# Second norm's columns by transposing transfers instead of TensorE, with logits one step later and the first and last steps reordered

## What is computed

```python
h = concat([tok(x), txt(x_txt)], axis=1)            # (64, 229, 128)
h = h + attn(layernorm(h))                          # gated attention, squared relu instead of softmax
t = layernorm(h)                                    # the second norm
shared = sum over 2 shared experts of gelu(t @ w1.T + b1) @ w2.T
logits = t @ gate_w.T + gate_b                      # 8 experts; softmax, top 2 of them
out = h + shared + sum over the top 2 of p_e * (gelu(t @ rw1[e].T + rb1[e]) @ rw2[e].T + rb2[e])
```

## Time and profile before

| | |
|---|---|
| median of 3 runs | 1225.05 us (1223.14 to 1229.79) |
| the profiled execution | 1222.94 us, of which its span is 1221.2 us |
| granted TensorE clock, mean | 0.991 of full speed |
| busy share | TensorE 95%, VectorE 80%, GpSimd 69%, ScalarE 66% |
| DMA traffic | 143.51 MB, 118 GB/s on average |

### The profile page before, as it was taken

How to read it: one execution, slowest core, us unless ns; L and a number is a source line. 1 busy time by engine, 2 the same in 40 slices (tenths; PEclk the granted TensorE clock), 3 DMA queues, 4 the chain that set the end, 5 groups by cost and what they waited for, 6 DMA issues and landing times.

```text
span 1221.2 us, 31914 instructions
## 1 busy us (share of the span) xinstructions
PE 1158.8 (95%) x9418; PEld 871.8 (71%) x9418; DVE 974.0 (80%) x2516; ACT 807.1 (66%) x1867; POOL 837.3 (69%) x808
## 2 busy tenths in 40 slices
PE   5899999999999999779999999999999999999998
PEld 3677777777777777654555458999999998965555
DVE  4688998888888888868977777777777766779997
ACT  2566656666765666645555547777777777768887
POOL 4335776666677777647878846777777777776664
PEclk9999999999999999989999999999999999999999
DMA  7134444444444442224344425554444544539998
GB/s 187 63 119 125 127 125 134 132 134 132 134 136 138 124 136 96 72 83 106 103 117 129 111 53 96 94 98 94 93 98 95 96 91 92 93 82 191 209 194 171
DMA packets 208055, 143.51 MB, mean 118 GB/s; under 512 B 119036, under 2 KB 186745, under 8 KB 207892
## 3 DMA queue, kind: packets, MB, share of 16 engines
q1 hardware_dynamic: 166868, 93.93, 30.6%
q0 software_dynamic: 36992, 40.97, 15.8%
q10 hardware_dynamic: 4032, 6.57, 2.1%
HBM read 70.38 MB, written 55.96 MB: 103 GB/s over the span
## 4 chain that ended last, share of the span: by engine, by line
PE 35%; POOL 34%; issue 21%; ACT 3%; SPq 2%; DVE 2%; DMA 2%; POOLq 0%; ACTq 0%; DVEq 0%
POOL slots_dram L487 9%; POOL slots_dram L1550 7%; PE bank L1838 4%; PE bank L1862 4%; PE bank L1861 4%; PE bank L1863 4%; PE bank L1840 4%; PE bank L1839 4%; POOL rstd L528 3%; POOL slots_dram L497 2%; POOL rstd L534 2%; POOL emb L457 2%; PE bank L1271 2%; PE bank L1310 2%; PE bank L1270 2%
## 5 line engine op out<-in xcount | busy, mean ns | idle before, releaser
L1561 POOL DMA_INDIRECT y_dram<-y_sb,y_row x244 | 268.8, 1102 | 98.3 <-issue 74.9
L1646 ACT ACTIVATE gel_all<-bank,b 128x256 f32<-128x256 f32 x488 | 191.4, 474 | 40.8 <-PE bank L1840 39.2
L1277 ACT ACTIVATE gel_all<-bank,b 128x458 f32<-128x458 f32 x256 | 154.4, 640 | 85.3 <-PE bank L1271 56.4
L1861 PE MATMUL bank<-w_part_hi,hid_all 128*128 x976 | 170.7, 219 | 0.0
L1863 PE MATMUL bank<-w_part_hi,hid_all 128*128 x976 | 169.7, 219 | 0.0
L1862 PE MATMUL bank<-w_part_lo,hid_all 128*128 x976 | 169.7, 219 | 0.0
L1768 DVE CAST hid_all<-gel_all 128x1024 f16<-128x1024 f32 x122 | 85.4, 700 | 97.4 <-ACT gel_all L1646 97.4
L487 POOL DMA_INDIRECT slots_dram<-row_bufs,slot_1st x128 | 131.8, 1030 | 41.0 <-issue 37.3
L1770 DVE TENSOR_TENSOR hid_all<-gel_all,hid_all 128x1024 f16<-128x1024 f32 x122 | 149.5, 1225 | 4.2
L1288 DVE TENSOR_TENSOR hid_all<-gel_all,hid_all 128x916 f16<-128x916 f32 x128 | 142.5, 1113 | 4.4
L1838 PE MATMUL bank<-xT_r,w_part_hi 128*128 128x256 f16 x488 | 133.3, 273 | 3.1 <-DMA tags_r<-slots_dram 2.8
(11 more groups left out here) (190 smaller groups left out, 3029.8 us busy)
## 6 DMA issues: line engine op xcount, KB each, us to landing
xin<-in_xmain SPq DMA_DIRECT2D x32, 771.8 KB
x2r_dram<-row_bufs SPq DMA_DIRECT2D x32, 260.0 KB, 2.1
x2t_dram<-x2T SPq DMA_DIRECT2D x32, 229.0 KB, 2.8
x_cols<-x2t_dram ACTq DMA_DIRECT2D x28, 229.0 KB, 3.2
row_bufs<-x2r_dram SPq DMA_DIRECT2D x24, 260.0 KB, 2.8
stage<-in_ffn_w SPq DMA_DIRECT2D x20, 256.0 KB
xin<-in_xrest SPq DMA_DIRECT2D x32, 128.6 KB
y_dram<-y_sb,y_row POOLq DMA_INDIRECT x244
```

The lines of the kernel that those rows point to most:

```text
L1561: pool.indirect_dma_start(out=y_dram, in_=y_sb[:, s, c, :], in_offset=None, out_offset=bass.IndirectOffsetOnAxis(ap=y_row[:, s, c:c + 1], ...
L1646: act.activation(gel[:, s8 % 2, f, :], up_bank[s8 % 2][half][:, (f % 2) * TILE:(f % 2 + 1) * TILE], ACT.Gelu, bias=of_expert(b1, SHARED * ...
L1861: pe.matmul(part, h_hi, w2_hi, start=False, stop=False)
```

## The change

The columns of the second norm no longer come from TensorE. `turn_x2` issues four transposing transfers per pair on SyncE's queue, from the fp16 row buffer in SBUF to the column tile in SBUF; the 128 transpositions of TensorE (`x2_columns`), 32 copies of ScalarE (`columns_hi`) and 32 subtractions of VectorE (`x2_low`) are gone. The block sizes swap to 112 and 117, and each image's columns get room for 240, so the column tile and its copy in DRAM grow from 458 to 480 numbers per row; `up` reads 2x229 of them. `halves_hi` and `halves_low` move ahead in their steps. `logits`, `top` and `choose` of a pair come one step later, `logits` stands right behind `av`; `rank` stays in its step, and `slots` moves to the end of VectorE's step. `top` gets two buffers (`mx8`). Steps -3 to -1 and 29 to 31 have orders of their own, with other pieces of the shared experts between them; TensorE turns `ident` 28 times while the first loads run, and ScalarE loads its Silu table at the start. VectorE's list behind step 30 is now: `halves_low(30)`, `middle(31)`, first `early.split`, `mid_shift(31)`, `top(29)`, `choose`, second `early.split`, `slots`, `halves_low(31)`, third `early.split`, `top(30)`, fourth `early.split`, `top(31)`, `choose`, `slots`. The core of the diff:

```diff
-CHUNKS = ((0, 117), (117, 112))
+CHUNKS = ((0, 112), (112, 117))
...
+IMG_COLS = CHUNKS[1][0] + P
+PAIR_COLS = 2 * IMG_COLS
+TURN_ROWS = (CHUNKS[0][1], P)
...
-            def store_x2(b, parity, buf):
+            def turn_x2(b, parity, buf):
+                if reaches(b, 2):
+                    sp.wait_ge(lg_done, b - 1)
+                    sp.wait_ge(t_out[parity], 8 * (b - parity))
                 sp.wait_ge(rows_ready, b + 1)
+                for img in range(2):
+                    for c, (at, _) in enumerate(CHUNKS):
+                        n, col = TURN_ROWS[c], img * IMG_COLS + at
+                        sp.dma_start(x2T16[:, parity, :, col:col + n], rows_16[0:n, buf, 2 * img + c, 0:2 * HID],
+                                     transpose=True).then_inc(x2_turned[parity], 16)
                 sp.dma_start(x2r_dram[b], rows_1st[:, buf]).then_inc(r_out[buf], 16)
-                sp.wait_ge(t_ready, b + 1)
+            def store_columns(b, parity):
+                sp.wait_ge(x2_turned[parity], 64 * (b // 2 + 1))
...
+                if exists(i - 2):
+                    store_columns(i - 2, p)
                 if exists(i - 1):
-                    store_x2(i - 1, 1 - p, (q - 1) % 4)
+                    turn_x2(i - 1, 1 - p, (q - 1) % 4)
...
-            steps(sp, step, PAIRS - 1)
+            steps(sp, step, PAIRS - 2)
             between(sp)
+            step(PAIRS - 2, 0, PAIRS // 2 - 1, 2)
             step(PAIRS - 1, 1, PAIRS // 2 - 1, 3)
             step(PAIRS, 0, PAIRS // 2, 0)
+            step(PAIRS + 1, 1, PAIRS // 2, 1)
...
-            def x2_low(b, parity):
-                dve.wait_ge(t_hi, b + 1)
-                dve.tensor_tensor(x2T16[:, parity, 1, :], tr2_bank[:, 0:PAIR_SEQ], x2T16[:, parity, 0, :],
-                                  ALU.subtract).then_inc(t_ready, 1)
...
-                if exists(i + 3):
+                if i == -3 or (i >= 0 and exists(i + 3)):
                     assemble(i + 3, 1 - p)
                 if not reaches(i, -2):
                     uvw_low()
+                    assemble(1, 1)
                 if exists(i):
                     gate(i, 1, p)
                 if exists(i + 2):
...
                 if exists(i - 1):
-                    x2_low(i - 1, 1 - p)
+                    halves_low(i - 1, (q - 1) % 4)
                 for img in range(2):
                     if exists(i + 1):
                         scores(i + 1, img)
                 if exists(i + 2):
                     xnT_low(i + 2, p)
-                if exists(i - 1):
-                    top(i - 1, 1 - p)
-                if exists(i - 1):
-                    halves_low(i - 1, (q - 1) % 4)
-                if p == 0 and exists(i - 2):
+                if exists(i - 2):
+                    top(i - 2, p)
+                if p == 1 and exists(i - 3):
                     choose(j - 1)
...
-                if p == 1 and exists(i - 3):
-                    slots(j - 1, (q // 2 + 1) % 2, 64 * ((j - 1) // 2) if isinstance(j, int) else 32 * j - (64 if q == 1 else 32))
                 if exists(i):
                     middle(i)
                     mid_variance(i)
+                if i == PAIRS - 4:
+                    gate(i + 1, 0, 1 - p)
                 if exists(i + 3):
                     front_stats(i + 3, 1 - p)
                     front_variance(i + 3)
-                if exists(i) and i < PAIRS - 2:
+                if exists(i):
                     mid_shift(i)
+                if p == 1 and exists(i - 3):
+                    slots(j - 1, (q // 2 + 1) % 2, 64 * ((j - 1) // 2) if isinstance(j, int) else 32 * j - (64 if q == 1 else 32))
+            def end_step(i, p, j, q):
+                if p == 1:
+                    gate(i, 1, p)
+                    front_scales(i + 2, p)
+                    front_norm(i + 2, p)
+                scores(i + 1, 0)
+                halves_low(i - 1, (q - 1) % 4)
+                scores(i + 1, 1)
+                if p == 1:
+                    xnT_low(i + 2, p)
+                    top(i - 2, p)
+                    choose(j - 1)
+                middle(i)
+                mid_variance(i)
+                gate(i + 1, 0, 1 - p)
+                mid_shift(i)
+                residual(i + 1, 1 - p)
+                gate(i + 1, 1, 1 - p)
+                if p == 1:
+                    slots(j - 1, (q // 2 + 1) % 2, 64 * ((j - 1) // 2))
+                else:
+                    top(i - 2, p)
...
+            act.wait_ge(tables, 1)
+            act.activation(silu_first[:, :], ident[:, 0:1], ACT.Silu)
...
                     second_norm(i - 1, (q - 1) % 4)
-                    if not drains(i):
-                        columns_hi(i - 1, 1 - p)
+                    halves_hi(i - 1, (q - 1) % 4)
                 for k in again_begins(i):
                     tag_again(k)
...
-                if reaches(n, 5):
-                    pe.wait_ge(lg_read, n - 4)
+                if reaches(n, 6):
+                    pe.wait_ge(lg_read, n - 5)
...
-            def x2_columns(b, buf):
-                pe.wait_ge(x2_ready, b + 1)
-                pe.wait_ge(xnT_ready, min(b + 3, PAIRS) if isinstance(b, int) else b + 3)
-                to_columns(x2_rows, tr3_done)
             def logits(b, parity):
                 if not reaches(b, 1):
                     pe.wait_ge(uvw_ready, 3)
-                pe.wait_ge(t_ready, b + 1)
-                pe.wait_ge(hT_ready, min(b + 5, PAIRS) if isinstance(b, int) else b + 5)
+                pe.wait_ge(x2_turned[parity], 64 * (b // 2 + 1))
+                pe.wait_ge(hT_ready, min(b + 6, PAIRS))
                 if reaches(b, 1):
                     pe.wait_ge(lg_read, b)
-                halves = x2T16[:, parity].rearrange("p h n -> p (h n)")
...
-                if exists(i - 1) and not drains(i):
-                    x2_columns(i - 1, (q - 1) % 4)
-                if exists(i + 3) and p == 1:
+                if exists(i - 2) and i != PAIRS - 2:
+                    logits(i - 2, p)
+                if exists(i + 3) and p == 1 and i != -1:
                     text(j + 2)
+                if i == -2:
+                    to_rows(1, 1, 0)
                 if exists(i + 1):
                     uv(i + 1, 1 - p, 1)
+                    if i == -1:
+                        uv(i + 1, 1 - p, 2)
                     qk(i + 1, 0)
-                    uv(i + 1, 1 - p, 2)
+                    if i != -1:
+                        uv(i + 1, 1 - p, 2)
                 if exists(i):
                     project(i, 0)
-                if exists(i - 1) and drains(i):
-                    x2_columns(i - 1, (q - 1) % 4)
+                if drains(i):
+                    qk(i + 1, 1)
+                    project(i, 1)
+                    if exists(i + 2):
+                        xn_columns(i + 2)
+                    uv(i + 1, 1 - p, 3)
+                    uv(i + 1, 1 - p, 4)
+                    if p == 1:
+                        rank(j - 1)
+                    else:
+                        logits(i - 2, p)
+                    return
                 if exists(i + 1):
                     qk(i + 1, 1)
+                if i == -1:
+                    text(j + 2)
                 if exists(i + 2):
                     xn_columns(i + 2)
-                if exists(i + 3):
+                if exists(i + 3) and i != -2:
                     to_rows(i + 3, 1 - p, j + (p + 3) // 2)
                 if exists(i):
                     project(i, 1)
                 if p == 1 and exists(i - 3):
                     rank(j - 1)
-                if exists(i - 1):
-                    logits(i - 1, 1 - p)
                 if exists(i + 1):
                     uv(i + 1, 1 - p, 3)
                     uv(i + 1, 1 - p, 4)
+            pe.wait_ge(tables, 1)
+            pe.wait_ge(setup_v, FIRST_BANKS)
+            for _ in range(WARM):
+                pe.transpose(tr1_bank[:, 0:P], ident[:, :], ident[:, :])
             pe.wait_ge(tokw_in, 32)
             pe.wait_ge(tables, 2)
-            pe.wait_ge(setup_v, FIRST_BANKS)
             steps(pe, step, PAIRS - 1)
             b = PAIRS - 1
+            between(pe, 0)
             av(b, 0)
             av(b, 1)
-            between(pe, 0)
+            between(pe, 1)
             project(b, 0)
             project(b, 1)
-            x2_columns(b - 1, (b - 1) % ROW_BUFS)
+            logits(b - 2, 1)
+            between(pe, 2)
             rank(GROUPS - 2)
+            between(pe, 3)
             logits(b - 1, 0)
-            between(pe, 1)
-            x2_columns(b, b % ROW_BUFS)
-            between(pe, 2)
+            between(pe, 4)
             logits(b, 1)
-            between(pe, 3)
+            between(pe, 5)
             rank(GROUPS - 1)
-            between(pe, 4)
-    done = Done(t_out, r_out, centred, exps, tagged, again_out, scattered, ws_done, top_kept, slots_up, mid_ready, sil, t_ready, routed, lg_read, w_late, b2_up)
+            between(pe, 6)
...
```

(64 more changed lines are left out.)

129 lines of the change are left out of this document (65 added, 64 removed).

## The result

The changed kernel takes 1242.72 us (median of 4 runs, 1241.54 to 1245.23), the kernel before 1225.95 (4 runs on record with it, 1223.14 to 1229.79). The ratio is 1.0137, with an interval of 1.0105 to 1.017: 1.4% slower, above the range that was given. The sign was wrong too.

What follows compares the result with a forecast made beforehand. TensorE was taken as the bound, VectorE 13% behind. 1222.94 - 6 (first steps) - 0.9 (early steps) + 8 (odd-step waits) - 8 (last steps) + 0.5 (column store) = 1216.5, taken as 1215 us; range 1194 to 1238.

Steps and rivals of the forecast that it cites:

- the second wait: TensorE at odd `patches` waits for `next_at`, which VectorE's `slots` makes: 0.3 us per odd step.
- the stretch: From the first `av` to the last pair's `patches`: +7 us forecast (8, less 0.9 for the early steps).
- The first wait: TensorE at `rank` in odd steps waits for `both` from VectorE's `choose`: 1.6 us each.
- the cover of the transposing transfers: On SyncE's queue, 1.22 us each, 4.9 per step, with 6 to 7 us of margin before logits: no cost.
- Rival 1: Odd steps: the waits are absorbed and the removed work counts fully; 1190 us, chance 0.18.
- Rival 2: Odd steps: the 1.6 us wait at `rank` lowers TensorE's clock, 20 us in all; 1235 us, chance 0.10.
- Rival 3: SyncE's queue: transposes of 4 us each make logits wait in every step; 1285 us and more, chance 0.09.
- rival 4: First and last steps: the edges give nothing and 8 us come back; 1223 us, chance 0.13.
- the start: First steps: reordering brings the first `av` from 43.79 to about 37 to 38; -6 us, between -4 and -8.
- the last steps: End of the attention stage: earlier `gate` places and shared experts fill TensorE's waits; -8 us, between -3 and -13.
- the 1216.5 of the sum: Whole kernel: 1222.94 - 6 - 0.9 + 8 - 8 + 0.5 = 1216.5 us, from which 1215 was forecast.
- the rival for slower: Rival 2: TensorE's clock falls behind the `rank` wait in odd steps; 1235 us, chance 0.10.

Runs made afterwards that it cites:

- e1: Changed kernel with VectorE's `slots` moved back ahead of `middle` in the odd steps; 1210.2 us, ratio 0.991 to the kernel before.
- e4: Changed kernel with six transposing transfers per pair in place of four for the first 28 pairs; 1242.16 us, ratio 1.0157 to the kernel before.
- e3: Changed kernel with `rank` behind the last two `uv` and `slots` right behind `mid_variance`; 1195.2 us, ratio 0.9779 to the kernel before.
- e2: Changed kernel with TensorE's `rank` moved behind the last two `uv` of the odd step; 1233.2 us, ratio 1.0088 to the kernel before.
- e9: Changed kernel with GpSimd's `mid_powers` ahead of the weights' low half and the second choices' row transfers; 1244.47 us, ratio 1.0168 to the kernel before.

## Why the prediction was wrong

- **The bound and the places were right.** TensorE sets the pace, the edit makes it wait for VectorE at `rank` and at odd `patches`, and the first `av` comes at 37.41, where 37 to 38 stood.
- **The term that failed is the second wait**, "from 290.70 to 294.80", which made "a wait of **0.3**". It was 1.5 us in plain steps and between none and 4.1 in those with second choices: 22.2 us where 0.3 x 12 = 3.6 stood, 19 of the 21 us by which the stretch was missed. e1, which takes this wait away alone, gives back 28 us. In the step at 300 us the distance from `middle` to `slots` was 5.46, not 4.10. The 4.10 were taken from a step where `mid_shift` waited for nothing. That it waits for GpSimd's `rstd` is in the code; what stands ahead of `rstd` on GpSimd (a weight half that hangs on ScalarE, and row transfers in later steps) was never worked out. The prediction used one step's timeline for all 13, and that step was one of the easy ones: in the same trace `mid_shift` waits 0.58 us for `rstd` in the odd step at 360.54 and 1.08 in the one at 392.78.
- **The first wait was right**: 1.59 us against 1.6. So was the cover of the transposing transfers: 1247 ns each at the median (1172 to 2671), where 1.22 us stood, and e4 shows two more of them hidden.

```profile
L397 SPq DMA_TRANSPOSE x2T<-row_bufs x128: 1172/1247/2671, 60.5 to 563.8; - x128
```

- The Trainium skill's table in "DMA: Bandwidth & Descriptors" ("Why a DMA increments its semaphore by 16 and not by 1"), which was weighed against this edit, does not decide here. From SBUF to SBUF a transfer of 112 or 128 rows took 1247 ns on the queue, one of the routed tiles from DRAM 1218.
- **Rival 1** (waits absorbed, 1190) is wrong for this kernel, but its price is near for e3, where the waits are taken away by hand: 1195 measured, and 1199 by the ratio and the 1225.95 us of the result. **Rival 2** (the clock) was right in kind, wrong in the place. Behind the 13 stops at `rank`, 1.6 us and once 2.41, the clock stayed at 1.00. It fell behind 4.05 and 2.81 us at `patches`, for some 4 us in all. Nor do these runs show a length of stop that decides. In e2 (the first two rows) the ten matmuls of `patches` took 3.53 us behind one stop of 2.38 us and 5.22 behind another; in e4 (the last two) they took 3.53 behind 2.79 us and 5.22 behind 1.96. What decides stays open. The prediction's argument against, that before only "waits of up to 0.3" left the clock at 1.00, was a wrong reading: in that stretch there are waits up to 0.97 us.

```profile
129.72 3.53 PE L1078 MATMUL bank<-xin,tokw 126*128 126x392 f32 x10 [2.38 <-DVE next_at L801]
291.32 5.22 PE L1078 MATMUL bank<-xin,tokw 126*128 126x392 f32 x10 [2.38 <-DVE next_at L801]
```

```profile
405.59 3.53 PE L1083 MATMUL bank<-xin,tokw 126*128 126x392 f32 x10 [2.79 <-DVE next_at L806]
471.44 5.22 PE L1083 MATMUL bank<-xin,tokw 126*128 126x392 f32 x10 [1.96 <-DVE next_at L806]
```

- **Rival 3** (SyncE's queue) and **rival 4** (the edges give nothing) are wrong: the start gave 6.4 us of 6, the last steps 6 of 8.
- **The sum mended**: to the 1216.5 of the sum come 21.1 in the stretch (19 the second wait, 4 the clock, less 2 of other terms, as added up above), 2.1 in the last steps, 2.3 behind the first routed tile (of it 1.9 waits for `tags_r`, 4.7 us against 2.8), and 0.4 go at the start. That is 1241.6, where the profiled execution took 1241.54. That no slower case held such a sum is the error of the range: the rival for slower had one mechanism with a doubt of its own, and the low price of the second wait had no upper end at all.

## What to carry to other kernels

When an instruction is moved behind others on its engine, the path to it holds their waits as well as their durations; walk each of those waits one engine further, in the busiest step as well as in a quiet one. Of two waits in a row on the bound engine, take away the later first (e1 gave 28 us, e2 6, both together 44 by the ratios). On an engine that waits often, work that fills a wait is free and the same work behind the wait is not: e9 took 15 us of one wait away and put 11 of another in its place.

## What was not expected of the hardware

A small VectorE instruction (`var`, 128x4) takes 0.17 us in most steps, but 0.69 in seven of the changed kernel's odd steps (0.34 and 0.54 in two more) and about 1.01 in 20 steps of e9. There GpSimd's `w_part_lo` is at work when it starts; in e9 that instruction begins 0.17 us ahead of it:

```profile
297.04 1.01 DVE L697 TENSOR_SCALAR var<-mv 128x4 f32<-128x4 f32 x1
```

```profile
296.87 1.14 POOL L497 TENSOR_TENSOR w_part_lo<-stage,w_part_hi 128x512 f16<-128x512 f32 x1
```

It ends when GpSimd's instruction does (298.01 and 298.05; 298.81 and 298.83 in the changed kernel), and so it does, within 0.1 us, in all 29 of these steps. The two engines seem to exclude each other for this pair of instructions, while VectorE's statistics (L676) beside the same work keep their length. It was seen in the traces and not tested by itself.
